# A recommendation tower on one core: layer 1 of the last tile of samples computed with its weights standing in TensorE

## The reference, cut to what matters

```python
e = stack([tbl_f[ids[:, f]] for f in range(26)], axis=1)           # 512 x 26 x 128
combined = concatenate([dense[:, None, :], e], axis=1)             # 512 x 27 x 128
z = einsum('bfd,bgd->bfg', combined, combined)[:, iu, ju]          # 512 x 351, pairs f < g
h = concatenate([z, dense], axis=1)                                # 512 x 479
h = maximum(h @ W_top1 + b_top1, 0)                                # 512 x 512
h = maximum(h @ W_top2 + b_top2, 0)                                # 512 x 256
y = h @ W_top3                                                     # 512 x 1
```

## Time and profile before

| what | us |
|---|---|
| median of 3 runs | 140.49 |
| the three runs | 139.82, 140.49, 142.6 |
| the profiled execution, its own time | 139.5 |
| its span, from the first to the last instruction | 137.5 |
| TensorE (PE) busy in the span | 115.6 |
| weight loads (PEld) busy in the span | 90.5 |
| DVE / ACT / POOL busy | 70.2 / 57.9 / 65.8 |

### The profile page before, as it was taken

How to read it: one execution, slowest core, us unless ns; L and a number is a source line. 1 busy time by engine, 2 the same in 40 slices (tenths; PEclk the granted TensorE clock), 3 DMA queues, 4 the chain that set the end, 5 groups by cost and what they waited for, 6 DMA issues and landing times.

```text
span 137.5 us, 3417 instructions
## 1 busy us (share of the span) xinstructions
PE 115.6 (84%) x1480; PEld 90.5 (66%) x1480; DVE 70.2 (51%) x123; ACT 57.9 (42%) x86; POOL 65.8 (48%) x63
## 2 busy tenths in 40 slices
PE   5999999999999839966182685679999998999992
PEld 4676688888888527744071574467878766877981
DVE  3799999999972644453000005115427413634342
ACT  3786994957803980054230040006535125215230
POOL 3889978787878778788477507640000000000000
PEclk9999999999999975555555558655899999999999
DMA  3999989999972361146112200210000000000000
GB/s 115 250 259 224 241 253 265 257 237 266 253 245 55 77 245 47 43 78 94 38 38 57 57 5 19 62 38 0 5 5 0 5 5 0 5 5 5 0 0 1
DMA packets 6028, 13.25 MB, mean 96 GB/s; under 512 B 1799, under 2 KB 2841, under 8 KB 6014
## 3 DMA queue, kind: packets, MB, share of 16 engines
q1 hardware_dynamic: 3162, 8.50, 23.8%
q0 software_dynamic: 1792, 3.67, 10.4%
q10 hardware_dynamic: 1060, 0.87, 2.5%
HBM read 13.02 MB, written 0.01 MB: 95 GB/s over the span
## 4 chain that ended last, share of the span: by engine, by line
PE 81%; issue 9%; another core or an unknown queue 3%; ACT 3%; DVE 2%; POOL 0%; POOLq 0%; DVEq 0%; ACTq 0%
PE banks L395 22%; PE banks L416 12%; PE banks L457 11%; PE banks L378 7%; PE banks L436 5%; PE banks L488 3%; PE banks L494 2%; PE banks L344 2%; PE banks L489 2%; PE banks L465 2%; PE banks L356 2%; DVE onehots L880 2%; PE banks L522 2%; PE banks L530 1%
## 5 line engine op out<-in xcount | busy, mean ns | idle before, releaser
L335 POOL DMA_INDIRECT rows<-in_tbl,ids_sb x56 | 65.0, 1160 | 24.7 <-issue 15.8
L395 PE MATMUL banks<-onehots,tab_hi 125*128 125x512 f32 x64 | 25.4, 397 | 0.6 <-issue 0.6
L395 PE MATMUL banks<-onehots,tab_lo 125*128 125x512 f32 x64 | 25.0, 390 | 0.0
L457 PE MATMUL banks<-feats 128*27 128x27 f32 x1024 | 16.6, 203 | 7.9 <-issue 7.6
L907 DVE COPY_PREDICATED picked<-second_of,banks 128x112 f32<-128x112 int32 x16 | 4.4, 282 | 35.9 <-ACT picked L752 35.9
L457 PEld LDWEIGHTS banks<-feats 128*27 128x27 f32 x1024 | 13.1, 114 | 14.0 <-issue 11.4
L416 PE MATMUL banks<-onehots,tab_hi 125*128 125x256 f32 x32 | 15.5, 487 | 8.1 <-issue 3.9
L880 DVE TENSOR_SCALAR onehots<-ids_bc_h,row_of 125x1024 fp32r<-125x1024 int16 x21 | 15.4, 769 | 8.4 <-PE banks L416 5.4
L752 ACT ACTIVATE picked<-banks 128x112 f32<-128x112 f32 x16 | 4.1, 261 | 34.4 <-PE banks L457 17.4
L416 PEld LDWEIGHTS banks<-onehots,tab_hi 125*128 125x128 f32 x32 | 9.6, 301 | 11.8 <-issue 5.5
L680 ACT ACTIVATE tab_hi<-stage 125x1024 fp32r<-125x1024 f32 (+1 forms) x12 | 12.0, 1022 | 12.6 <-PE banks L395 8.5
(11 more groups left out here) (89 smaller groups left out, 152.3 us busy)
## 6 DMA issues: line engine op xcount, KB each, us to landing
stage<-in_tbl SPq DMA_DIRECT2D x11, 448.0 KB
stage<-in_w SPq DMA_DIRECT2D x3, 512.0 KB
rows<-in_tbl,ids_sb POOLq DMA_INDIRECT x56
ids_bc_h<-ids_short_rows ACTq DMA_DIRECT2D x6, 128.0 KB
stage<-in_tbl SPq DMA_DIRECT2D x11, 52.0 KB
stage<-in_tbl SPq DMA_DIRECT2D x2, 224.0 KB
dense_sb<-in_dense SPq DMA_DIRECT2D x1, 256.0 KB
stage<-in_w SPq DMA_DIRECT2D x1, 256.0 KB
```

What stands on the lines that cost most here:

```text
L335: nc.gpsimd.indirect_dma_start(out=rows[:, t % RB, m, :], out_offset=None, in_=tables[m], in_offset=bass.IndirectOffsetOnAxis(ap=ids_sb[:, ...
L395: last = nc.tensor.matmul(bank(n, k), tab_part(i, part)[:, c, :], onehots[0:RP, c, k, :], start=(c == 0 and part == 0), stop=(c == CHUNKS ...
L457: last = nc.tensor.matmul(gram_ps(u)[SLOT * s:SLOT * s + F, i, 0:F], x, x, start=True, stop=True)
```

## The change

Layer 1 of the last tile changes its operands' places: a 128x128 piece of the weights stands, and the 128 samples move. The sums of 128 output features come with the features on the partitions, in four groups m = 0 to 3, in the banks 6, 0, SPARE (the bank of the last group of turned rows) and 1. So the four transposes of the last tile's hidden layer, and its copy in `h1`, go: ACT takes the maximum from the bank straight into `h1T_hi`, and DVE makes `h1T_lo` in one instruction from the bank. `l2_last` moves from bank 1 to bank 2. Layer 2 of the last tile is issued by group, and `layer2_lo(T - 2)` stands earlier in TensorE's list.

```diff
-    turns += [(T - 2, None), moved(T - 1), (T - 1, 0, None), (T - 1, 1, None)]
+    turns += [(T - 2, None), moved(T - 1)]
+    SPARE = bank_of[-3]
-        l2_last = banks[:, 1, :]
+        l2_last = banks[:, 2, :]
-        def l1_half(e):
-            return l1_ps[:, 0:HH] if e == 0 else banks[:, 0, 0:HH]
+        def last_l1(m):
+            return banks[:, (6, 0, SPARE, 1)[m], 0:P]
...
-                    pe.wait_ge(picked_by_dve, U * t + 3)
+                    pe.wait_ge(picked_by_dve, U * t + 4)
...
             def last_layer1_dense():
                 pe.wait_ge(h1_ready, T - 1)
-                dense_products(T - 1, l1_half(0), slice(0, HH))
-                pe.wait_ge(picked_by_dve, U * (T - 1) + 2)
-                dense_products(T - 1, l1_half(1), slice(HH, H1))
+                for m in range(C1):
+                    if m == 1:
+                        pe.wait_ge(picked_by_dve, U * (T - 1) + 2)
+                    elif m == 2:
+                        pe.wait_ge(turn_by_dve, dve_turns(len(turns) - 2))
+                    elif m == 3:
+                        pe.wait_ge(picked_by_dve, U * (T - 1) + 3)
+                    cols = slice(P * m, P * (m + 1))
+                    nc.tensor.matmul(last_l1(m), w1_at(0, 0, cols), dense_hi[:, T - 1, :], start=True, stop=False)
+                    nc.tensor.matmul(last_l1(m), w1_at(0, 0, cols), dense_lo[:, T - 1, :], start=False, stop=False)
+                    nc.tensor.matmul(last_l1(m), w1_at(1, 0, cols), dense_hi[:, T - 1, :], start=False, stop=False)
...
-            def last_layer1_hi(e):
+            def last_layer1_hi(m):
                 pe.wait_ge(pairs_hi_ready, T)
-                cols = slice(HH * e, HH * (e + 1))
+                cols = slice(P * m, P * (m + 1))
                 for k in range(1, NK + 1):
                     x = pairs_hi[(T - 1) % 2][:, k - 1, :]
-                    nc.tensor.matmul(l1_half(e), x, w1_at(0, k, cols), start=False, stop=False)
-                    nc.tensor.matmul(l1_half(e), x, w1_at(1, k, cols), start=False, stop=False)
+                    nc.tensor.matmul(last_l1(m), w1_at(0, k, cols), x, start=False, stop=False)
+                    nc.tensor.matmul(last_l1(m), w1_at(1, k, cols), x, start=False, stop=False)
...
-                    last = nc.tensor.matmul(l1_half(e), pairs_lo[(T - 1) % 2][:, k - 1, :], w1_at(0, k, cols),
+                    last = nc.tensor.matmul(last_l1(m), w1_at(0, k, cols), pairs_lo[(T - 1) % 2][:, k - 1, :],
                                             start=False, stop=(k == NK))
...
-            def last_transpose_hidden(e):
...
+            def last_layer2(m):
+                x_hi, x_lo = h1T_hi[(T - 1) % 2][:, m, :], h1T_lo[(T - 1) % 2][:, m, :]
+                pe.wait_ge(last_hi_ready, m + 1)
+                nc.tensor.matmul(l2_last[:, 0:H2], x_hi, w2_hi[:, m, :], start=False, stop=False)
+                nc.tensor.matmul(l2_last[:, 0:H2], x_hi, w2_lo[:, m, :], start=False, stop=False)
+                pe.wait_ge(last_lo_ready, m + 1)
+                last = nc.tensor.matmul(l2_last[:, 0:H2], x_lo, w2_hi[:, m, :], start=False, stop=(m == C1 - 1))
...
             last_layer1_hi(0)
             last_layer1_lo(0)
+            layer2_lo(T - 2, l2_ps[:, 0:H2])
             last_layer1_hi(1)
-            last_transpose_hidden(0)
             last_layer1_lo(1)
-            layer2_lo(T - 2, l2_ps[:, 0:H2])
-            last_transpose_hidden(1)
             layer2_start(T - 1, l2_last[:, 0:H2])
-            layer2_hi(T - 1, l2_last[:, 0:H2], range(0, CH))
-            layer2_lo(T - 1, l2_last[:, 0:H2], range(0, CH))
-            layer2_hi(T - 1, l2_last[:, 0:H2], range(CH, C1))
-            layer2_lo(T - 1, l2_last[:, 0:H2], range(CH, C1))
+            last_layer1_hi(2)
+            last_layer1_lo(2)
+            last_layer2(0)
+            last_layer1_hi(3)
+            last_layer1_lo(3)
+            last_layer2(1)
+            last_layer2(2)
+            last_layer2(3)
...
+            def last_hidden_hi(m):
+                act.wait_ge(layer1_done, T + m)
+                if m == 0:
+                    act.wait_ge(layer2_done, T - 2)
+                nc.scalar.activation(h1T_hi[(T - 1) % 2][:, m, :], last_l1(m), ACT.Relu).then_inc(last_hi_ready, 1)
...
-            last_relu1(0)
-            hidden_hi(T - 1, 0)
-            last_relu1(1)
-            hidden_hi(T - 1, 1)
+            for m in range(C1):
+                last_hidden_hi(m)
...
+            def last_hidden_lo(m):
+                dve.wait_ge(last_hi_ready, m + 1)
+                nc.vector.scalar_tensor_tensor(h1T_lo[(T - 1) % 2][:, m, :], last_l1(m), 0.0,
+                                               h1T_hi[(T - 1) % 2][:, m, :].bitcast(f32), ALU.max,
+                                               ALU.subtract).then_inc(last_lo_ready, 1)
...
-            hidden_lo(T - 1, 0)
             finish(T - 2)
-            hidden_lo(T - 1, 1)
+            for m in range(C1):
+                last_hidden_lo(m)
             finish(T - 1)
```

## The result

The changed kernel takes 143.6 us (median of 4 runs, 142.54 to 145.56), the kernel before 141.07 us beside it (139.82 to 142.6). The ratio is 1.0202, with a 95% interval of 1.014 to 1.0265: slower by 2.0 to 3.7 us, 142.3 us was forecast. The ratios leave out runs in a slower state that some executions of either kernel show, so they are not the quotients of the medians. All three intervals hold 1.02: whether the change costs more or less than 2% is not decided.

The account below looks back on a forecast made before the run. PE was taken to bound the kernel after 126.23. Work that stays (3.66 us) plus the new layer 1 (6.60) gave 10.26 against 8.44, +1.8 us; put on the 140.49 us median, 142.3 us, range 139.3 to 144.3.

Parts of the forecast that it names:

- The bound: After 126.23, PE is busy nearly throughout at full clock; a microsecond of PE work moves the end by a microsecond.
- What was added: Last tile's layer 1 becomes 60 products of 128 columns instead of 30 of 256: 6.60 us against 3.54.
- p: Pitch of f32r products of 128 columns in the last tile's layer 1, taken as 0.11 us, set by the weight load.
- What was removed: The L568 transposes, 0.66 us of PE, and the gap of 0.18 if the dense products outlast it.
- the gap of 0.18: PE's idle 0.18 us between the last tile's dense products and `move_picked`, forecast to fall to 0.
- What stays: `move_picked` 0.63, `layer2_hi(T - 2)` 0.94, `layer2_lo(T - 2)` 0.47, bias product 0.12, layer 2 1.40 plus tail 0.1: 3.66 us.
- the sum: Stretch from the last tile's first dense product to the last `finish`: 3.66 + 6.60 = 10.26 us against 8.44, +1.8 us.
- The other edits: Bank moves, pair waits, ACT maxima, DVE order and the end were all claimed to be hidden behind PE's work.
- The forecast's 0.25: At the end, 0.69 us of ACT and DVE to `h1T_lo` against 0.94 us of PE products: covered by 0.25.
- the load hides: Rival in layer 1: pitch 0.058 us, stretch 7.32, -1.1 us, 139.4 us; chance 0.19, wholly or half hidden.
- a narrow f32r product runs like plain f32: Rival in layer 1: pitch 0.22 us, stretch 16.86, +8.4 us, 148.9 us; chance 0.19.
- this mechanism alone: The load sets layer 1's pitch: 142.3 us, own range 141.6 to 143.3 with p from 0.10 to 0.12; chance 0.62.

Follow-up runs that it names:

- All three intervals: Changed kernel against the kernel before, timed on three chips: ratios 1.0202 (1.014 to 1.0265), 1.0207 (1.0134 to 1.0279), 1.0198 (1.015 to 1.0246).
- Half: Changed kernel with its 60 layer-1 products of the last tile moving 64 of 128 samples: stretch 13.28 us, 146.13 us in all; repeated on another chip, 13.29 us.
- twice: Changed kernel with each of the 60 layer-1 products of the last tile moving 256 columns: stretch 10.98 us, pitch 0.118.
- samples standing: Kernel before, samples still standing and transposes kept, last tile's layer 1 cut into 60 products of 128 weight columns: stretch 11.49 us, 146.27 us in all.
- the half-clock stream: Changed kernel with layer-1 products moving 64 columns, after its clock fell to the 1.2 GHz level: pitch 0.21 us, stretch 13.28 us.

## Why the prediction was right

**The bound.** Right: PE at full clock without a gap, and every microsecond of PE work moved the end. The stretch and the timed difference agree within the intervals.

**What was added.** Right: p = 0.11 was taken, 0.111 measured as a mean over the 60 products. The step that carried it was to read the distance between the starts of two loads with nothing moving in between, and not the length of a load's record (0.19 us) nor the columns (0.058). Half, twice and samples standing show from three sides that the number of loads and products is the price, not the columns or the operand that stands. That it is the load and not the pair as such is read from rows 4 and was not tested.

**What was removed.** Right: with the transposes alone taken out the stretch fell by 0.76 us against 0.66, of which 0.10 came in layer 1, and in the changed kernel the gap of 0.18 closed.

**What stays.** Here the size was off by 0.17 us net; with the 0.06 of layer 1 that is 0.23, the whole error of the sum. The bias product was put at 0.12 "since it now stands inside a stream": it cost 0.31 as before, and 0.15 more in the layer-1 product behind it. The reason is its 2 rows, not its surroundings. `move_picked` was 0.17 cheaper: in 0.63 the load of its first transpose had shown, which had waited for DVE. Layer 2 with its tail cost 1.61 for 1.50: the two products that follow a 128-column product took 0.17 us in place of 0.12 (L576 at 136.61 and 138.30). So the small net error is partly luck: 0.34 us too little for the bias product and the one behind it stand against 0.17 too much for `move_picked`.

**The other edits.** Right: no wait on a bank, on `pairs_hi` or `pairs_lo`. At the end the last subtraction ran from 138.64 to 138.93 and its product started at 139.13: 0.20 later. The forecast's 0.25 already had a hop of 0.05 taken off, so on its count 0.15 was left.

```profile
138.33 0.28 ACT L755 ACTIVATE tab_hi<-banks 128x128 fp32r<-128x128 f32 x1 [1.41 <-PE banks L569]
...
138.64 0.29 DVE L946 SCALAR_TENSOR_TENSOR tab_lo<-banks,tab_hi 128x128 fp32r<-128x128 f32 x1 [1.40 <-ACT tab_hi L755]
...
139.13 0.28 PE L579 MATMUL banks<-w_hi,tab_lo 128*128 128x256 f32 x1
```

ACT's and DVE's costs, estimated as 0.28 and 0.30, were 0.28 and 0.29.

**The rivals.** That the load hides fell with the pitch, and its argument with the half-clock stream: the 0.17 us that a lone load shows at half clock is less than what a load occupies in a stream (0.21), so splitting 0.11 and 0.17 into a fixed and a clocked part said nothing of streams. That a narrow f32r product runs like plain f32 (0.22 us) fell with the measured pitch of 0.111. That 128 columns run at half the rate of 256, which would also give 0.11, fell with the 64 columns, which cost no less than 128. The Trainium skill's 81 ns for a pair of load and product at 128 columns ("TensorE: Matmul & The Clock Gate", "Back-to-back issue gap") was not reached with f32r, 0.11 us measured. The same page of the Trainium skill, in the section "LDWEIGHTS (loading the stationary operand)", gives a load's time in ns as its columns divided by 1.2, for 128 columns an estimate of 107 ns. For f32r at the 2.4 GHz level the trace agrees (0.11 us); at the 1.2 GHz level it is 0.21, and the loads of plain f32 transposes start 0.06 us apart at 2.4 GHz.

**The size.** The forecast was +1.8 us and the stretch gave +2.05. The median moved by 2.5 on the first chip; what lies above 2.05 is within its interval and was not attributed. The median of 143.6 lies 0.3 above the 141.6 to 143.3 that the prediction gave for this mechanism alone; the kernel before came out at 141.07 beside it, not at 140.49. The last `finish` started at 139.51 and not near 136.5, since the stretch began 2.79 us later in the profiled run. And the prediction gave 0.68 to a difference within 2%; the ratios lie at 2% and leave that open.

## What to carry to other kernels

Count weight loads before columns: here an f32r product with 128 loaded columns cost 0.11 us at full clock with 64 or 128 columns moved, and 0.12 with 256. So fewer than 256 moving columns are paid nearly as 256. Turning a product round to save a transpose pays only if it doesn't double the loads: layer 1 cost 3.12 us more, and 0.66 us of transposes, the gap of 0.18 and 0.17 of `move_picked` were saved. And pad a product of very few rows to the rows of its neighbours: a 2-row bias product among 128-row ones cost 0.3 us more than a padded one.

## What the runs showed of the hardware that was not expected

- The granted clock fell from 1.00 to 0.50, the 1.2 GHz level, in the middle of a stream in which the records show PE and PEld busy without a gap: in both runs of the kernel whose layer-1 products move 64 columns, on two chips, one of which kept 1.00 everywhere else. In the runs of the same stretch with 128 or 256 columns it stayed at 1.00. It cost 2.8 us here (13.28 against 10.49).
- A product over 2 rows is not overlapped with 128-row neighbours on either side (0.31 + 0.26 us for it and the next, against 0.17 + 0.06 over 128 rows).
- The kernel before takes 141 us where the granted clock falls in its middle (0.84 over the span) and about 107.5 us on two other chips. The changed kernel's two timed runs there have profiles with 1.00 throughout. The chain that ended last differs between them: 57% through POOL's gathers in the first (upper line), 92% through PE in the second. So what bounds the shared part at full clock is not settled:

```profile
POOL 57%; PE 19%; issue 15%; DMA 4%; POOLq 1%; DVE 1%; DVEq 0%
...
PE 92%; issue 2%; DVE 2%; ACT 1%; POOL 0%; POOLq 0%; DVEq 0%
```

- Why the clock falls on some chips in the shared part, and not on others, no run here tells.
